# A chain of convolutions: x loaded and y stored in strided transfers of 16 channels instead of one transfer per window

## What is computed

```python
x = x + conv3x3(_gn(x), w0) + bias               # A: zero padding       -> "x1"
x = x + newton_inverse(_gn(x), 5)                # B: each 128x128 plane as a matrix -> "x2"
x = x + circular_conv3x3(_gn(x), w2)             # C: written with FFTs in the reference
x = x + conv3x3(_gn(x), w3) * mask               # D: last row and last column not added -> y
```

## Time and profile before

| | us |
|---|---|
| median of 3 runs | 797.71 |
| lowest, highest | 796.5, 798.39 |
| the profiled execution's own time | 802.89 |
| its span in the trace | 801.1 |

### The profile page before, as it was taken

How to read it: one execution, slowest core, us unless ns; L and a number is a source line. 1 busy time by engine, 2 the same in 40 slices (tenths; PEclk the granted TensorE clock), 3 DMA queues, 4 the chain that set the end, 5 groups by cost and what they waited for, 6 DMA issues and landing times.

```text
span 801.1 us, 11705 instructions
## 1 busy us (share of the span) xinstructions
PE 625.7 (78%) x3752; PEld 523.5 (65%) x3752; DVE 534.0 (67%) x1304; ACT 384.4 (48%) x559; POOL 198.3 (25%) x289
## 2 busy tenths in 40 slices
PE   0776689449995889949897689949997697997766
PEld 0555678348774778748775677748776576887544
DVE  3765685567874778756784778746884569647561
ACT  0333255315655357624666256734666243754542
POOL 5132123022321225211241224312241213210312
PEclk9997799869998899969999799979999698999888
DMA  5233013401442232411452132521332231513431
GB/s 147 50 104 96 17 40 98 137 16 49 113 160 58 74 82 90 149 53 53 112 168 65 48 100 74 167 60 57 73 112 90 69 82 36 161 39 72 129 96 52
DMA packets 88632, 69.11 MB, mean 86 GB/s; under 512 B 6974, under 2 KB 81630, under 8 KB 86654
## 3 DMA queue, kind: packets, MB, share of 16 engines
q1 hardware_dynamic: 87054, 66.73, 29.0%
q0 software_dynamic: 1536, 1.86, 0.9%
HBM read 23.46 MB, written 16.91 MB: 50 GB/s over the span
## 4 chain that ended last, share of the span: by engine, by line
PE 40%; DVE 25%; SPq 17%; DMA 8%; issue 5%; ACT 5%; POOL 0%; DVEq 0%; ACTq 0%
PE conv_ps L681 21%; SPq L286 13%; DMA x<-x 5%; DVE zl L935 5%; PE z L770 4%; PE z L761 3%; PE z L763 3%; PE z L765 3%; SPq L275 3%; DVE stB L607 2%; DVE bn_D L469 2%; PE z L756 2%; DMA x<-out_A 2%; ACT d_A L581 2%; PE spare_ps L781 1%
## 5 line engine op out<-in xcount | busy, mean ns | idle before, releaser
L935 DVE SCALAR_TENSOR_TENSOR zl<-z,zh 128x1024 fp32r<-128x1024 f32 x128 | 154.4, 1219 | 66.9 <-ACT zh L868 64.3
L761 PE MATMUL z<-zh 128*128 128x256 f32 x512 | 160.0, 312 | 14.5 <-DVE zl L935 14.5
L868 ACT ACTIVATE zh<-z 128x1024 fp32r<-128x1024 f32 x128 | 130.4, 1020 | 71.1 <-PE z L765 37.7
L763 PE MATMUL z<-zl,zh 128*128 128x256 f32 x512 | 151.9, 297 | 0.0
L765 PE MATMUL z<-zh,zl 128*128 128x256 f32 x512 | 151.5, 296 | 0.0
L761 PEld LDWEIGHTS z<-zh 128*128 128x128 f32 x512 | 106.0, 207 | 23.9 <-DVE zl L935 20.7
L681 PE MATMUL conv_ps<-d_A,w_D 128*96 128x512 f32 (+1 forms) x432 | 105.5, 394 | 16.9 <-DVE w_D L539 16.0
L681 PE MATMUL conv_ps<-d_C,w_C 128*96 128x512 f32 (+1 forms) x486 | 114.2, 382 | 0.7 <-issue 0.6
L681 PE MATMUL conv_ps<-d_A,w_A 128*96 128x512 f32 (+1 forms) x378 | 98.1, 410 | 14.8 <-DVE w_A L539 10.8
L763 PEld LDWEIGHTS z<-zl,zh 128*128 128x128 f32 x512 | 105.8, 207 | 1.1
L765 PEld LDWEIGHTS z<-zh,zl 128*128 128x128 f32 x512 | 105.3, 206 | 0.0
(11 more groups left out here) (182 smaller groups left out, 940.3 us busy)
## 6 DMA issues: line engine op xcount, KB each, us to landing
win_C<-rows_dram SPq DMA_DIRECT2D x40, 256.0 KB, 4.0
win_A<-x SPq DMA_DIRECT2D x132, 64.0 KB
x<-x SPq DMA_DIRECT2D x8, 1024.0 KB, 5.5
rows_dram<-x SPq DMA_DIRECT2D x32, 256.0 KB
y<-out_D SPq DMA_DIRECT2D x160, 48.0 KB
win_D<-out_C SPq DMA_DIRECT2D x7, 1056.0 KB, 6.8
x<-out_A SPq DMA_DIRECT2D x139, 48.0 KB
win_D<-out_C SPq DMA_DIRECT2D x14, 160.0 KB, 5.9
```

The lines of the kernel that those rows point to most:

```text
L761: pe.matmul(z[s][:, m, :], zh[s][:, m, 0:128], zh[s][:, m, :], start=False, stop=True, skip_group_check=True)
L763: pe.matmul(z[s][:, m, :], zh[s][:, m, 0:128], zl[s][:, m, :], start=False, stop=True, skip_group_check=True)
L868: act.activation(zh[s][:, :, :], z[s][:, :, :], ACT.Copy, scale=ROOT[j]).then_inc(s_zh[s], 1)
L935: dve.scalar_tensor_tensor(zl[s][:, :, :], z[s][:, :, :], ROOT[j], zh[s][:, :, :].bitcast(f32), ALU.mult, ALU.subtract).then_inc(s_zl[s], 1)
```

## The change

x is loaded, for images 2 to 7, by `load_x_rows`: for each of the eight rows r of a window one transfer, which fills partitions 16 r to 16 r + 15 (the 16 channels) of windows 1 to 20, from DRAM in pieces of one image row of 512 B that lie six rows apart; the first and the last window are loaded as before. That is 10 transfers in place of 22. All of them wait until the low parts of all six groups of the image before are made. (`load_x` is left for images 0 and 1.)

y of images 0 to 6 is stored by `store_y_rows`: six such transfers of 16 partitions x 21 windows and one for the last window, after all six groups of `out_D` are there. The last row of y, which comes from `out_C`, is now stored right behind `windows_from_windows` of its own image, a cycle earlier than before. The last image's y is stored as before, with a semaphore of its own.

The 22 transfers of `rows_from_windows` are as they were.

```diff
--- before.py
+++ after.py
@@ -230,6 +230,7 @@
         s_ycol = sem("y_column_ready")
         s_y = sem("y_stored")
         s_yrow = sem("y_last_row_stored")
+        s_y_sp = sem("last_y_stored_by_sp")
         s_y_pool = sem("y_stored_by_pool")
         s_first, s_last = sem("first_window_fixed"), sem("last_window_fixed")
         s_tail = [sem(f"last_win_D{p}_loaded") for p in range(3)]
@@ -247,7 +248,8 @@
         n_xs = NCHK + 2
         n_x2 = NG + 1
         n_x3 = 5
-        n_y = NBLK
+        n_y = OUT_ROWS + 1
+        n_xd = WIN + 2
 
         def is_int(b, n):
             return isinstance(b, int) and b == n
@@ -256,6 +258,23 @@
 
             return at(16 * n_x1, b, -16 * n_x1_pool)
 
+
+        def by_row(t, b, first, n):
+
+            one = t[bass.ds(b, 1), :, first:first + 1, :]
+            return bass.AP(tensor=one.tensor, offset=one.offset, ap=[[H * W, C], [OUT_ROWS * W, n], [1, W]])
+
+        def load_x_rows(sp, b):
+
+            sp.wait_ge(cA.s_dl, NG if is_int(b, 2) else at(NG, b))
+            for r in range(WIN):
+                sp.dma_start(cA.win[C * r:C * (r + 1), 1:NBLK - 1, :],
+                             by_row(x, b, window_row(1) + r, NBLK - 2)).then_inc(cA.s_win, 16)
+            for k in (0, NBLK - 1):
+                h0 = window_row(k)
+                lo, hi = max(h0, 0), min(h0 + WIN, H)
+                sp.dma_start(cA.win[(lo - h0) * C:(hi - h0) * C, k, :],
+                             x[bass.ds(b, 1), :, lo:hi, :].rearrange("b c h w -> (b h) c w")).then_inc(cA.s_win, 16)
 
         def load_x(eng, b, g):
 
@@ -265,9 +284,6 @@
             elif is_int(b, 1):
                 done = s_xsp1 if g in SP_X else s_xpool1
                 eng.wait_ge(s_zero, 2)
-            else:
-                done = cA.s_win
-                eng.wait_ge(cA.s_dl, NG if is_int(b, 2) else at(NG, b - 1, g + 1))
             k0, kn = SPLIT_G[g]
             for k in range(k0, k0 + kn):
                 h0 = window_row(k)
@@ -365,15 +381,27 @@
             sp.dma_start(w[(WIN - 1) * C:, last - 1, :], o[below * C:(below + 1) * C, last, :])\
                 .then_inc(s_tail[-1], 16)
 
-        def store_y(sp, b, groups=range(NG), done=None):
-
-            done = done or s_y
+        def y_rows(b, lo, hi):
+            return y[bass.ds(b, 1), :, lo:hi, :].rearrange("b c h w -> (b h) c w")
+
+        def store_y_last_row(sp, b):
+
+            sp.dma_start(y_rows(b, H - 1, H), cC.out[OP - C:OP, NBLK - 1, :]).then_inc(s_yrow, 16)
+
+        def store_y_rows(sp, b):
+
+            sp.wait_ge(cD.s_out, at(NG, b, NG))
+            sp.wait_ge(s_ycol, at(1, b, 1))
+            for r in range(OUT_ROWS):
+                sp.dma_start(by_row(y, b, r, NBLK - 1), cD.out[C * r:C * (r + 1), 0:NBLK - 1, :]).then_inc(s_y, 16)
+            first = FULL - (LAST_ROW + 1)
+            sp.dma_start(y_rows(b, FULL, H - 1), cD.out[first * C:OP - C, NBLK - 1, :]).then_inc(s_y, 16)
+
+        def store_y(sp, b, groups, done):
 
             def rows(lo, hi):
-                return y[bass.ds(b, 1), :, lo:hi, :].rearrange("b c h w -> (b h) c w")
+                return y_rows(b, lo, hi)
             wait(sp, s_ycol, at(1, b, 1))
-            if 0 in groups:
-                sp.dma_start(rows(H - 1, H), cC.out[OP - C:OP, NBLK - 1, :]).then_inc(s_yrow, 16)
             for g in groups:
                 k0, kn = SPLIT_G[g]
                 wait(sp, cD.s_out, at(NG, b, g + 1))
@@ -395,14 +423,14 @@
                 for g in range(NG):
                     rows_from_windows(sp, i + 1, g)
             if has_D:
-                store_y(sp, i - 2)
+                store_y_rows(sp, i - 2)
             store_x2(sp, i, 0)
             store_x2(sp, i, 1)
             if has_C:
                 windows_from_windows(sp, i - 1)
+                store_y_last_row(sp, i - 1)
             if load:
-                for g in range(NG):
-                    load_x(sp, i + 3, g)
+                load_x_rows(sp, i + 3)
             store_x2(sp, i, 2)
             store_x2(sp, i, 3)
             store_x2_edges(sp, i)
@@ -462,7 +490,7 @@
                 elif c is cA and is_int(b, 0) and part < 2:
                     dve.wait_ge(*((s_x0, 16 * windows_of(SP_X)), (s_x0p, 16 * windows_of(POOL_X)))[part])
                 elif c is cA and part == 0:
-                    dve.wait_ge(cA.s_win, at(16 * NBLK, b, -16 * NBLK))
+                    dve.wait_ge(cA.s_win, at(16 * n_xd, b, -16 * n_xd))
                 for j in (range(3), range(3, 6), range(6, last))[part]:
                     if c is cD:
                         dve.wait_ge(cC.s_out, at(NG, b, (3 * j + 2) // SPLIT_G[0][1] + 1))
@@ -1243,15 +1271,16 @@
                 load_x(sp, 1, g)
             for g in SP_ROWS:
                 rows_from_windows(sp, 0, g)
-            for g in range(NG):
-                load_x(sp, 2, g)
+            load_x_rows(sp, 2)
             cycles(sp, sp_cycle)
             for g in range(NG):
                 load_x2(sp, B - 1, g)
-            store_y(sp, B - 2)
+            store_y_rows(sp, B - 2)
             windows_from_windows_last(sp)
-            store_y(sp, B - 1, SP_Y)
-            sp.wait_ge(s_y, 16 * (n_y * B - windows_of(POOL_Y)))
+            store_y_last_row(sp, B - 1)
+            store_y(sp, B - 1, SP_Y, s_y_sp)
+            sp.wait_ge(s_y_sp, 16 * windows_of(SP_Y))
+            sp.wait_ge(s_y, 16 * n_y * (B - 1))
             sp.wait_ge(s_yrow, 16 * B)
 
         @block.gpsimd
```

## The result

The changed kernel takes 837.77 us (median of 4 executions, 837.51 to 839.23) where the one before, beside it, takes 797.89: a ratio of 1.0506, 95% interval 1.0488 to 1.0525, that is 39.9 us slower. The forecast was 824 us, in a range of 803 to 845. The sign, the place and the way were as written; the size of one term was not.

The account below looks back on a forecast made before the run. Bound by the chain x2 stored, reloaded as windows, x1 kept, x1's rows moved, stB. Five later reloads cost 27.3 us, less 0.6 at the start: +26.7 on the median of 797.71 gave 824 us, range 803 to 845.

Parts of the forecast that it names:

- The path: Each cycle is set by x2 stored, reloaded as windows, x1 kept, x1's rows moved, stB; later x2 stores move everything after.
- T: End of the last low part, made by POOL; 403.86 in cycle 3, from which the reload's start is counted.
- y: On SP's queue, fewer y stores free some 15 us earlier, in slack; the new wait costs nothing: worth 0.
- The wait of SP, x's transfers all behind the last low part: All 1.43 MB and ten issues fall into the 5.75 us before x2's last slice, ahead of x2's stores and reload.
- The issue is not what costs: Ten x loads on SP issue in about 6.3 us at 0.59 each, less than the 9.8 us of data.
- The price of a boundary: Reload begins at T + 13.7, eight narrow transfers taking 9.4 us; costs 6.4, 5.5, then 5.2 three times, 27.3 us in all.
- my own case: Eight narrow x transfers at 140 GB/s; range 814 to 834 us for rates 180 to 115 GB/s; chance 50%.
- rival 2: Narrow x transfers slower still, 94 to 110 GB/s, from pieces of 512 B: 837 to 847 us; chance 15%.
- One of my signs of being wrong: Wrong if reload begins by T + 10, win_D's first-row rate fails for DRAM loads, or keep_x1 doesn't move with the reload.
- The copy "lands when the reload's bytes in front are through": keep_x1, behind the x2 reload on SP, lands 10.0 to 10.1 us after the reload began, so stC's microsecond gives no cover.
- The start: Ten loads of image 2 instead of 22 bring x1's rows about 6 us earlier; stB gains only 0.6 us.
- The end: Image 6's later y stores delay the last window moves to near 773.3; their reader begins at 776.53, covered by 3 us.

Follow-up runs that it names:

- late_wide: Kernel before, with each of its 22 x loads of 128 partitions waiting for the low parts of all six groups: 862.41 us, 1.0815.
- early_rows: Changed kernel, with x windows 1 to 15 loaded in eight narrow transfers after group 3's low part, the other seven windows singly: 800.87 us, 1.0032.
- half_bytes: Changed kernel, same ten x loads at the same place, but the eight rows for windows 1 to 10 only: 803.47 us, 1.0076.
- sbuf_spread: Changed kernel, each narrow x transfer writing partitions r, r + 8, ... r + 120 instead of 16 neighbours: 818.03 us, 1.026.
- dram_adjacent: Changed kernel, the 16 partitions of each narrow x transfer reading 16 adjacent image rows instead of rows 64 KB apart: 837.15 us, 1.0505.
- Experiment 6: Kernel before, with keep_x1 issued ahead of the reload of x2 instead of behind it: 806.67 us, 1.0132.
- y_only: Changed kernel without its x part: y stored the new way, x loaded in 22 transfers as before: 796.73 us, 1.0001.

## Why the prediction was right, and where it fell short

**The path: right for the changed kernel.** x2 stored, reloaded, x1 kept, rows moved, `stB`; every delay of the reload passed through. Added up over the five boundaries with loads, the reload begins later behind T by 8.7 (143.16 - 127.17 against 7.33), 8.4, 7.3, 7.7 and 7.9 us: 40.0 us, and 39.9 were measured. Cycles 5 to 7 gave nothing, as written. For the kernel before, the prediction had the path wrong from cycle 1 on: there `stC` released the copy, about 1 us behind the reload's last issue. This microsecond was no cover in cycle 3 all the same, because the copy took 1.0 us longer behind the later reload (6.12 against 5.08 us): x1's rows begin 7.6 us later behind T, the reload 7.7.

**y: right.** Worth 0, run alone 1.0001.

**The wait of SP, x's transfers all behind the last low part: right,** and `late_wide` (late and wide) and `early_rows` (early and narrow) show that it is what costs.

**The issue is not what costs: right.** It was even cheaper than the 0.59 us I took, 0.48, and `half_bytes` left it and lost the price.

**The price of a boundary: the step that was mis-sized is the rate of the eight narrow transfers.** I took 140 GB/s, the mean of two stretches of `windows_from_windows`, 9.4 us. It was 104 to 119, about 12 us for loads that begin 1.5 us behind T. T + 13.7 became T + 15.9 to 16.7. With the bytes' time corrected by 2.5 us at five boundaries the forecast would have been 837. My two stretches were mixed: they began while the 96-partition transfer before was still running out (the first half microsecond of the second has 280 GB/s), and so showed a mean over a wide and a narrow part. The Trainium skill's SBUF — State Buffer, section "Door 1: The DMA port swizzle", had the better number with its 104 GB/s, and I had it beside the sum as an estimate of 841. The measured 837.77 lies outside my own case, 814 to 834, and inside rival 2, 837 to 847, to which I gave 15%: by the rate rival 2 is what happened, though not for the reason I gave it (pieces of 512 B in series), since `sbuf_spread` moves the same pieces at 195, and `dram_adjacent` shows that the distance between their sources has no part in it. One of my signs of being wrong came true as well: the rate of win_D's first row did not carry over to loads from DRAM.

**The copy "lands when the reload's bytes in front are through": not as put.** The 10.0 to 10.1 us from reload to landing came again in cycle 3 of the changed kernel (438.01 to 447.99), but it was 11.5 at cycle 0 to 1, and about 11 at cycle 1 to 2 of the kernel before (232.34 + 6.2 against 227.59). Experiment 6 gives the reason no support: with no reload in front of it the copy took 5.7 to 5.9 us and not 4.5.

**The start: right in size.** `stB` of cycle 0 begins at 81.62, 0.52 us earlier, and DVE waits for nothing there now. The copy lands no earlier than before, in effect: it is issued at 50.03 instead of 58.52 and lies behind 1.4 MB of narrow loads, so that x1's rows begin at 62.30 instead of 63.08. The 6 us that I gave SP's rows were 0.8.

**The end: right.** The moves of the last windows begin at 803.21 and their reader 8.2 us later, as before (8.7).

**The profiled execution of before** was itself late: its T in cycle 0 is at 129.94, where `y_only`, which is the same there, has 127.48 and the changed kernel 127.17. The spans of the two profiles differ by 34.8 us, the medians by 39.9; the boundaries, each measured from its own T, are free of this.

## What to carry to other kernels

Before transfers are merged, ask what their old waits bought: 22 small loads that trickled out as their space came free cost nothing at 77 GB/s, and ten quick ones behind the last of these waits stood with all their bytes ahead of the one store that the next stage waits for. A queue's busy share says nothing of this; the time between an issue and the wait that ends on it does. And count a transfer's partitions on the SBUF side: loads into 16 neighbours took 104 to 120 GB/s wherever they read (stores from 16 neighbours 153), where transfers of 128 partitions went at 292. A "bigger" transfer can so be more than two times slower per byte than a wide one. Where a price has to be read from a stretch that holds two shapes, take the slower end of it.

## What was not expected of the hardware

The same 16 x 20 pieces of 512 B went at 119 GB/s to 16 neighbouring partitions and at 195 to 16 that lie eight apart; moving their sources in DRAM from 64 KB apart to adjacent changed nothing (837.15 against 837.77 us). Two such rows in flight on two queues were no faster than one after the other (110 GB/s). The spread transfer was dearer to issue, 0.74 against 0.48 us.
